# Last group of an attention kernel: where PE waits for the values, and where gamma and tanh of the last token tile stand

## The reference, cut to what matters

```
xn = layernorm(x)
q, k, v = xn @ wq + bq, xn @ wk + bk, xn @ wv + bv      # rope on q and k
s = softmax(q k^T / 4) v                                # 32 heads, 4 share k and v
z = xn @ W^T + b
m = sum over experts of p_e * (xn @ A_e) @ B_e          # rank 128 in all
gamma = min(0.5 * |z| / (|m| + 1e-6), 1)                # one number for each token
out = x + s * silu(z + gamma * m)
```

## Time and profile before

| | us |
|---|---|
| median of 3 runs (438.16 to 438.51) | 438.49 |
| the profiled execution | 436.62 |
| its span (first to last event of the profile) | 434.8 |
| PE busy, share of the span | 420.0, 97% |
| DVE busy | 370.9, 85% |
| ACT busy | 310.1, 71% |
| POOL busy | 138.3, 32% |
| mean granted clock of PE, 1 being full | 0.985 |

### The profile page before, as it was taken

One profiled execution on the slowest core, in us unless ns is written; L12 is line 12 of the kernel. 1 busy time (PEld: TensorE's weight loads), 2 busy tenths in 40 slices (PEclk: granted clock), 3 DMA queues, 4 the chain that ended last, 5 costly groups with the idle time before them and its releaser, 6 DMA issues.

```text
span 434.8 us, 8295 instructions
## 1 busy us (share of the span) xinstructions
PE 420.0 (97%) x3153; PEld 182.1 (42%) x3153; DVE 370.9 (85%) x613; ACT 310.1 (71%) x612; POOL 138.3 (32%) x195
## 2 busy tenths in 40 slices
PE   7999999998999999999999999999999999899993
PEld 3647333333444344444444444444434444333330
DVE  5844798998999999999999999999999999623443
ACT  2231111227889889999999899999989989766882
POOL 7972332444004030511313040322304030401554
PEclk9999999997899999999999999999999999999997
DMA  8949995444000010000000000000000000020002
GB/s 261 310 107 127 133 120 84 62 75 73 4 2 2 21 39 3 2 2 2 4 2 2 2 2 4 2 3 0 3 4 2 3 0 4 3 87 2 21 23 67
DMA packets 13624, 18.09 MB, mean 42 GB/s; under 512 B 3168, under 2 KB 7552, under 8 KB 13584
## 3 DMA queue, kind: packets, MB, share of 16 engines
q1 hardware_dynamic: 12064, 16.44, 20.0%
q10 hardware_dynamic: 1520, 1.12, 0.9%
HBM read 6.72 MB, written 2.10 MB: 20 GB/s over the span
## 4 chain that ended last, share of the span: by engine, by line
PE 86%; POOL 3%; DVE 3%; issue 2%; ACT 2%; DMA 2%; SPq 0%; DVEq 0%; POOLq 0%; ACTq 0%
PE st L1122 32%; PE oT L1090 27%; PE st L934 6%; PE sm L1197 3%; PE oT L1173 3%; PE oT L934 3%; PE sm L1038 2%; PE sm L1013 2%; PE sm L1099 2%; DMA x_sb<-in_x 2%; PE st L1154 2%; PE st L963 2%; POOL arena L466 1%; DVE negmax L795 1%; PE sm L1203 1%
## 5 line engine op out<-in xcount | busy, mean ns | idle before, releaser
L803 DVE TENSOR_REDUCE neghalf<-sm 128x1 f32<-128x512 f32 x448 | 270.9, 680 | 1.5 <-PE sm L1013 1.2
L709 ACT ACTIVATE arena<-st 128x512 f32<-128x512 f32 x448 | 233.0, 600 | 21.1 <-PE st L1122 16.4
L1013 PE MATMUL sm<-kA,qA 48*128 48x512 f32 x448 | 158.1, 446 | 0.0
L1122 PE MATMUL st<-qA,kA 50*128 50x512 f32 x448 | 154.9, 442 | 1.4 <-DVE z_sb L846 1.1
L1090 PE MATMUL oT<-arena,vg 128*32 128x256 f32 (+3 forms) x1568 | 129.7, 423 | 0.0
L1122 PEld LDWEIGHTS st<-qA,kA 50*128 50x128 f32 x448 | 74.0, 186 | 98.7 <-ACT arena L709 82.1
L537 POOL TENSOR_TENSOR rsum<-junk,consts 128x16 f32<-128x16 f32 x13 | 37.9, 2913 | 127.9 <-ACT junk L681 127.9
L1013 PEld LDWEIGHTS sm<-kA,qA 48*128 48x128 f32 x448 | 74.1, 186 | 2.6 <-DVE neghalf L803 2.1
L1090 PEld LDWEIGHTS oT<-arena,vg 128*32 128x32 f32 x1568 | 33.5, 109 | 46.7 <-issue 42.4
L795 DVE TENSOR_REDUCE negmax<-sm 128x1 f32<-128x1024 f32 x32 | 37.9, 1218 | 7.0 <-PE sm L1038 7.0
L730 ACT ACTIVATE arena<-st 128x512 f32<-128x512 f32 x48 | 27.0, 602 | 14.6 <-PE st L1154 14.6
(11 more groups left out here) (122 smaller groups left out, 360.2 us busy)
## 6 DMA issues: line engine op xcount, KB each, us to landing
qA<-arena SPq DMA_DIRECT2D x45, 128.0 KB, 5.1
x_sb<-in_x SPq DMA_DIRECT2D x8, 256.0 KB, 5.8
kA<-qA SPq DMA_DIRECT2D x12, 128.0 KB, 6.6
wT_sb<-in_wT SPq DMA_DIRECT2D x1, 1024.0 KB, 7.5
out<-x_sb SPq DMA_DIRECT2D x1, 896.0 KB, 4.1
out<-x_sb SPq DMA_DIRECT2D x4, 224.0 KB, 2.0
z_sb<-in_wq SPq DMA_DIRECT2D x1, 768.0 KB, 10.0
qA<-qA SPq DMA_DIRECT2D x3, 128.0 KB, 3.8
```

Source lines behind the costliest of these rows:

```text
L709: act.activation(probs[:, s % PB, h, :], st[:, st_score(0, s, h) % 3, :], ACT.Exp, scale=float(D) ** -0.5).then_inc(st_free, 1)
L803: dve.tensor_reduce(neghalf[:, e // 16, e % 16, j % 2:j % 2 + 1], sm[:, n % 4, :], AX.X, ALU.max, negate=True).then_inc(sm_free, count)
L1013: pe.matmul(sm[:, n % 4, :], qA[rows, half, g // 2, h, qt * P:(qt + 1) * P], kA[rows, g // 2, kh * HALF:(kh + 1) * HALF], start=True, stop ...
L1122: pe.matmul(st[:, n % 3, :], kA[rows, g // 2, kt * P:(kt + 1) * P], qA[rows, half, g // 2, h, :], start=True, stop=True).then_inc(st_full, 1)
```

## The change

Three moves. No instruction that computes is added or removed.

- PE: the wait for `v_ready` of group 7 goes from the start of `last_group`, ahead of its first scores, to `last_block`, ahead of the first piece of values that reads them.
- POOL: `gamma(7)` goes ahead of `add_late(6)`.
- ACT: the tanh of tile 7 goes ahead of the last copy of heads.

```diff
@@ -582,8 +582,8 @@
             gamma(6)
             add_late(5)
             finish(LAST, 0, LAST, z_sb)
+            gamma(7)
             add_late(6)
-            gamma(7)
             add_late(7)
@@ -735,8 +735,8 @@
                 if s in (7, 10, 13):
                     gate_tanh_of({7: 4, 10: 5, 13: 6}[s])
+            gate_tanh_of(7)
             evacuate(last_values(2 * NT - 1), 1, (m_full, LAST_BANK_M.index("out1") + 1))
-            gate_tanh_of(7)
@@ -1168,6 +1168,8 @@
                 if tiles[0] % NT == 0:
                     pe.wait_ge(heads_out, 2 * LAST + tiles[0] // NT)
+                if tiles[0] == 0:
+                    pe.wait_ge(v_ready, LAST + 1)
@@ -1206,7 +1208,6 @@
             def last_group():
 
                 pe.wait_ge(low_in, 48)
-                pe.wait_ge(v_ready, LAST + 1)
```

## The result

| | before | after |
|---|---|---|
| median | 438.34 us (4 runs, 438.16 to 438.51) | 433.44 us (4 runs, 432.91 to 434.95) |
| profiled execution / its span | 436.62 / 434.8 | 434.95 / 433.1 |
| mean granted clock of PE in it | 0.985 | 0.988 |

The ratio is 0.9894, 95% interval 0.9869 to 0.9919: faster by 4.9 us in the medians. Two things want an explanation: the two profiled executions differ by only 1.7 us, and the medians by 4.9.

What follows compares the result with a forecast made beforehand. The prediction took PE, with 86% of the chain of waits, as the bound: 1.97 us from the hole at 376 plus 1.35 from the tail, 3.3 off the median of 438.49, gives 435.2 us, range 434.4 to 436.6.

Steps and rivals of the forecast that it cites:

- Part 1: PE's idle hole at 376 us, before the last group's first scores: moving the v_ready wait removes all 1.97 us.
- Rival B: Hole at 376 us has another last releaser and stays, whole (437.1 us) or by half (436.15); 7%.
- Part 2: POOL near the end: gamma(7) ahead of add_late(6) ends at 423.33, gate_sum(7) at 424.15; add_late(6)'s delay is hidden.
- its collision: DVE and POOL side by side: gate(6) may hold gamma(7) by 0.69 us, gate_sum(7) may add 0.4 to add_late(6).
- Part 3: ACT's idle 1.18 us after the last Exp: tanh fits, gate(7) leaves the path, 0.18 us by itself.
- The tail: Behind PE's last transposes: add_late(7) runs earlier, DVE's L914 and L916 shorten, last store goes 1.35 us sooner.
- the landing: After the last store is issued: the time it takes to land was left as it is.
- rival A: DVE's last two operations keep their length; the hole's 1.97 goes, the tail gives 0.27: 436.25 us; 12%.
- the carried difference: Whole-kernel time: the median's 1.87 us above the profiled execution was carried over unchanged.
- Rival D: Last group, ACT-paced stretch after 382.67: PE's clock falls, 8 us cost 3.4, time 438.6 us; 3%.

Runs made afterwards that it cites:

- experiment 5: Kernel before, wait in place, plus two dense PE matmuls whose result nobody reads in the idle hole at 376 us: 437.19 us against 439.03, ratio 0.9975.
- 6: Kernel before with only gamma(7) moved ahead of add_late(6) on POOL: 438.68 us against 439.03, ratio 1.0015.
- 7: Kernel before with only the tanh of tile 7 moved ahead of the last copy of heads on ACT: 438.43 us, ratio 0.9994.
- experiment 1: The kernel before again, no edit, for a second profile and many times: 438.49 us, ratio 0.9997.
- 11: Kernel before with add_late(7) on POOL treating 16 columns instead of 448, so the output is incomplete: 435.82 us, a single execution.
- 3: Kernel before with only gamma(7) and the tanh of tile 7 moved, the v_ready wait left in place: 437.26 us, ratio 0.9965.
- 2: Kernel before with only the wait for v_ready moved: 435.37 us, ratio 0.9941.
- 4: The changed kernel again, no edit: 433.29 us, ratio 0.9884 to the kernel before.
- 12: Changed kernel plus two unread f32 matmuls at 100.2 us and one unread bf16 matmul behind each of group 0's first seven score pairs: 432.90 us, ratio 0.9868.
- 10: Kernel before plus two unread powers of 128x8 on POOL ahead of group 7's values, lengthening PE's hole to 5.18 us: 443.02 us against 438.65, ratio 1.0114.
- experiment 8: Changed kernel plus two unread f32 matmuls in PE's idle 1.09 us before group 0's first scores: 433.53 us, ratio 0.9888 to the kernel before.
- 13: Kernel before plus two unread f32 matmuls at 100.2 us and one unread bf16 matmul behind each of group 0's first seven score pairs: 438.31 us, ratio 0.9995.
- 9: Changed kernel plus two unread matmuls at 100.2 us and one of 128x128 behind each of group 0's first six score pairs: 433.93 us, ratio 0.9894.

## Why the prediction missed: point by point

**Part 1, the hole: right.** 1.97 us gone, released by L517 (named in experiment 5), nothing late behind it, the first reader 9.2 us clear of its values (9.4 forecast). Rival B is out.

**Part 2, gamma: right, its collision in the wrong place.** gamma(7) ends at 423.89. Adding the 0.08 by which PE's last pieces stand later, the forecast was 423.4 alone and 424.1 with gate(6) in the way; L489 shows the hold (0.71 instead of 0.23). At the next meeting I had POOL held by DVE for 0.4. It was DVE that was held: L817 took 1.62 and ended at 425.55, not 424.9. The slack covered it, with 0.6 us left before ACT was free.

**Part 3, tanh: right.** It runs in ACT's gap from 426.18 to 426.83, the copy starts 0.07 behind PE as before. Experiments 6 and 7 show that neither move works alone.

**The tail: right in mechanism, 0.4 too small in size.** Forecast 1.35, measured 1.53 at the last issue and 0.24 behind it. Two terms were off. PE's transposes took 0.63 and not 0.86: the profile of before had the lower clock there (the granted clock of its last 11 us is 0.70), while its repetition in experiment 1 had 0.63 too. Before, the tail took 5.9 with either length; after, the last operations follow the transposes, so their length counts. And I left the landing as it was. DVE held by POOL was the right reading (experiments 7 and 11), so rival A is out. Here the rule in the Trainium skill ("SBUF — State Buffer", section "Who interferes with whom") and the traces agree: 0.42 us with POOL idle, 1.23 with POOL reading SBUF.

**The step that failed: "The median of the runs is 438.49, 1.87 above the profiled one, and I carry the difference over unchanged."** I took 1.87 us as an offset between two kinds of runs. About 1.2 of it was what the change removes. The executions of the kernel before spread over 9 us (436.32 to 445.34), and its profiled ones lay at the low end each time. The spread comes for the larger part from PE's hole: in some executions the clock falls behind it and the first dense units of the last group run at half speed (experiments 3 and 7). Taking the idle time out of the hole, with or without the wait, brings the median nearer to the lowest time (2, 4, 5, 12); lengthening it makes the cost regular (10). So the gain is about 3.7 us by the traces (3.5 between the lowest times) and, in the median, 1.2 more. The miss of 1.8 us is then 1.2 for the carried difference, 0.4 for the tail, and the rest the median of before, 438.34 in the result instead of 438.49. With the tail's 0.4 alone the time would have lain in the range.

Rival D had the mechanism, a fall of PE's clock in the last group, and the wrong sign. Its place was the ACT-paced stretch after 382.67, and the spells of experiments 3 and 7 lie ahead of it, at 379.2 to 382.6 and 380.2 to 383.6; its price was 3.4 us, and they cost 1.7. I saw that the clock had stayed at 1.00 behind the hole in one trace and took it as evidence that holes there are harmless. One trace shows one execution. The nearest rows, a shorter idle time at 100.5 with a fall behind it, said the opposite.

**What stays open.** The executions of 438.5 to 439.5 in experiment 5, and the one of 438.68 in experiment 8, have another cause, which no profile caught. Which executions get a spell behind the hole I can't say: of seven profiles with a hole of 2 us two show it, of seven without one none. No profile caught an execution of 440 us or more, so that its time, too, comes from a spell behind the hole is inferred from the mean clocks and from experiments 5, 10 and 13. How the 1.2 divides between spells of different length wasn't measured.

## What to carry to other kernels

An idle stretch of PE in mid-kernel can have two prices, as it had here: its length, and the chance of a low-clock spell in the dense work behind it. Read the second from the list of executions (times beside mean clocks), since one profile shows one draw; when the median lies well above the profiled execution, look for what differs before carrying the difference over. At the tail, look where two engines' SBUF operations meet, and judge moves on several engines together: a value needed earlier wins nothing until its reader stands earlier too.

## What the hardware showed beyond expectation

- The same idle time doesn't always lower the clock. At 376 it fell 1.6 and 1.8 us behind the end of a hole of 1.97 us in two of seven profiles; near 104 it fell in all eleven profiles with 1.09 us of idle time ahead, followed by scores at ACT's pace. With that idle time filled it still fell (experiment 8); with matmuls between the scores as well it didn't (9, 12, 13).
- A DVE operation with two SBUF inputs issued 0.08 us behind a POOL operation of 1.15 us took 1.62 instead of 0.75.
- A small f32 matmul (128x128) between scores cost 0.36 us, a bf16 one of 128x256 0.16 (pairs at 0.85 and 0.65 instead of 0.49).
- A power of 128x8 on POOL took 1.6 us, where I had counted 1.25 to 1.5.
